# A two-layer attention and feed-forward kernel: first feed-forward on rows sorted by expert, later queries beside the second attention

## The reference

```python
x = x + _L0_xattn_ref(_layernorm(x), ctx_2048, itok, ...)
x = x + _L0_ffn_ref(_layernorm(x), router_w, gate_up_w, down_w, shared_gate_w, shared_up_w, shared_down_w)
x = x + _L1_xattn_ref(_layernorm(x), ctx_2048, wq, bq, wkv, bkv, wp, bp)
x = x + _L1_ffn_ref(_layernorm(x), W_up, W_down, W_gate, W_expert)

def _L0_ffn_ref(...):                       # E = 8 experts, K = 2, I = 128
    shared = silu(x @ shared_gate_w) * (x @ shared_up_w) @ shared_down_w
    top_val, top_idx = top_k(x @ router_w, K)
    probs = zeros_like(logits).at[arange(T)[:, None], top_idx].set(sigmoid(top_val))
    xin = probs.T[:, :, None] * x[None]
    gate, up = split(einsum('etd,edf->etf', xin, gate_up_w), 2, axis=-1)
    return shared + einsum('eti,eid->etd', silu(gate) * up, down_w).sum(axis=0)

def _L1_xattn_ref(x, cond, ...):            # 16 heads of 16
    q = qdq(x) @ qdq(wq).T + bq             # qdq: int8 fake quantisation by row
    ...
```

## Time and profile before

| | us |
|---|---|
| median of 3 runs | 811.05 (809.56 to 811.33) |
| the profiled execution, its own time | 809.53 |
| its span, first to last instruction | 807.6 |
| PE busy | 751.5 (93%) |
| DVE busy | 566.8 (70%) |
| ACT busy | 383.5 (47%) |
| POOL busy | 197.8 (24%) |
| mean granted clock of PE | 0.987 |

### The profile page before, as it was taken

How to read it: one execution, slowest core, us unless ns; L and a number is a source line. 1 busy time by engine, 2 the same in 40 slices (tenths; PEclk the granted TensorE clock), 3 DMA queues, 4 the chain that set the end, 5 groups by cost and what they waited for, 6 DMA issues and landing times.

```text
span 807.6 us, 13086 instructions
## 1 busy us (share of the span) xinstructions
PE 751.5 (93%) x5026; PEld 425.8 (53%) x5027; DVE 566.8 (70%) x1290; ACT 383.5 (47%) x562; POOL 197.8 (24%) x208
## 2 busy tenths in 40 slices
PE   7999899979989889789999999999999999899996
PEld 3445677856556556544444455554455554345434
DVE  3967988633455765687788787767787777887814
ACT  2101434445423233236666666556665566564670
POOL 1397322323721311210400504100505002200000
PEclk9999999999999999999999999999999999999999
DMA  9300001105589143144083391630491810550000
GB/s 294 138 0 1 1 1 27 57 1 185 113 146 138 62 60 47 22 60 79 1 145 40 117 135 16 142 55 2 150 116 62 115 23 1 117 69 14 1 2 13
DMA packets 32473, 55.90 MB, mean 69 GB/s; under 512 B 11572, under 2 KB 20532, under 8 KB 31509
## 3 DMA queue, kind: packets, MB, share of 16 engines
q1 hardware_dynamic: 32408, 55.04, 34.6%
HBM read 42.56 MB, written 12.46 MB: 68 GB/s over the span
## 4 chain that ended last, share of the span: by engine, by line
PE 64%; DVE 23%; issue 6%; POOL 3%; ACT 2%; DMA 1%; SPq 0%; DVEq 0%; POOLq 0%; ACTq 0%
PE ps L1111 12%; PE ps L1000 12%; PE ps L1090 9%; PE ps L888 5%; PE ps L898 5%; DVE small L1679 5%; PE ps L944 3%; PE ps L964 3%; POOL r L623 2%; PE ps L814 2%; PE ps L857 2%; PE ps L845 2%; DVE small L1629 1%; DVE r L1598 1%; DVE r L1605 1%
## 5 line engine op out<-in xcount | busy, mean ns | idle before, releaser
L1679 DVE TENSOR_REDUCE small<-ps 128x1 f32<-128x400 f32 (+1 forms) x512 | 286.0, 573 | 81.5 <-PE ps L1000 75.4
L1490 ACT ACTIVATE r<-ps 128x1024 f32<-128x1024 f32 (+1 forms) x208 | 212.6, 1024 | 89.0 <-PE ps L1090 86.1
L1000 PE MATMUL ps<-r 96*128 96x400 bf16 (+1 forms) x512 | 171.0, 341 | 13.7 <-DVE small L1679 10.9
L651 POOL TENSOR_TENSOR r<-r 128x401 bf16<-128x401 f32 (+3 forms) x96 | 87.8, 949 | 204.3 <-ACT r L1331 203.2
L1111 PE MATMUL ps<-r 128*17 128x256 f32 (+1 forms) x1664 | 130.7, 386 | 2.3 <-ACT r L1490 2.0
L1090 PE MATMUL ps<-r 99*128 99x256 bf16 (+1 forms) x832 | 125.8, 273 | 0.0
L1000 PEld LDWEIGHTS ps<-r 96*128 96x128 bf16 x512 | 49.5, 97 | 125.8 <-DVE small L1679 92.6
L1090 PEld LDWEIGHTS ps<-r 99*128 99x128 bf16 (+1 forms) x832 | 81.4, 99 | 31.5 <-issue 9.3
L944 PE MATMUL ps<-r,hT 128*128 128x512 f32 (+1 forms) x160 | 68.4, 559 | 0.0
L898 PE MATMUL ps<-wkvT,r 128*128 128x256 f32 (+1 forms) x208 | 57.0, 392 | 0.0
L1111 PEld LDWEIGHTS ps<-r 128*17 128x17 f32 (+1 forms) x1664 | 27.7, 95 | 52.0 <-issue 41.4
(11 more groups left out here) (199 smaller groups left out, 966.9 us busy)
## 6 DMA issues: line engine op xcount, KB each, us to landing
r<-kscr SPq DMA_DIRECT2D x96, 200.1 KB, 8.9
kscr<-r SPq DMA_DIRECT2D x24, 400.2 KB, 3.5
r<-in_ctx_dram SPq DMA_DIRECT2D x4, 1601.0 KB, 6.7
r<-qscr SPq DMA_DIRECT2D x24, 128.0 KB, 4.9
r<-in_wo_dram SPq DMA_DIRECT2D x1, 2048.0 KB, 13.5
r<-in_gu_dram SPq DMA_DIRECT2D x1, 2048.0 KB, 7.7
qscr<-qpart SPq DMA_DIRECT2D x24, 64.0 KB, 1.7
x<-in_x_dram SPq DMA_DIRECT2D x1, 1024.0 KB, 5.3
```

Source lines behind the costliest of these rows:

```text
L651: last = nc.gpsimd.tensor_tensor(into[:, a:a + n], kf[s][:, a:a + n], of[:, a:a + n], ALU.subtract)
L1000: mm(bank(ca % 2)[:, 0:m], qst[0:SROWS, h, q0:q0 + P], kst[0:SROWS, s % 2, h % HALF, a:a + m], start=True, stop=True).then_inc(mx_mm, 1)
L1490: fn(pr[i % 3][0:n, :], bank(2 + 2 * (i % 2), 2)[0:n, :], ACT.Exp, scale=SCALE1)\
L1679: v.tensor_reduce(mxc[quad % 2][:, n:n + 1], bank(ca % 2)[:, 0:m], AX_X, ALU.max).then_inc(mx_rdy, 1)
```

## The change

**First feed-forward.** Each row goes to its two experts only. Two groups are sorted apart: tiles 0 and 1, and tiles 2 to 7. For each group PE transposes and routes all its tiles, DVE takes the top two and writes a one-hot membership, PE multiplies it by a triangular matrix and by ones (the rank of each row within its expert, and the counts), and DVE works out each row's two positions in a list where each expert starts at a multiple of 128 (`choose`, `place`). ACT makes two scaled copies of each row, with the sigmoid as scale. POOL scatters them by indirect DMA into a DRAM buffer (`send`) that is cleared at the program's start. The list has 11 and 19 blocks of 128 rows, the most that 256 and 768 rows can need with two experts each, 30 together, and all 30 are always computed. DVE also writes each block's expert times 256 (`owner_at`).

SP loads the blocks in 15 pairs through three buffers (`load_sorted`) and stores results through four (`store_sorted`). The items are those 15 pairs and four shared ones (two tiles each). In step n, PE does gate-up of item n (for a pair after loading the two owners into registers, which select the weights' columns), the transposition of the next pair, the down product of item n-2 and the hidden transposition of item n-1. ACT does silu for both blocks and the copies, DVE the product and the evacuation. A row's two results come back by indirect gathers on POOL (`fetch`), and DVE adds them to x (`join`).

**Queries.** They go by batch. Batch 0's stand beside the items 12 to 16. Those of batches 1, 2 and 3 go into the second attention's table, with joins in steps 0, 4 and 9 and the rest from steps 1, 25 and 77. The values of batch 1 and the first quad's maxima stand beside the steps from 18 and 19 on.

**Keys.** The splits of stages 0 and 1 move from POOL to DVE (three passes of 1601 columns each, in the steps 1 to 4). Their writing and the stacking of quads 0 and 1 move from SP to POOL; the stacking of quads 2 and 3, and the rows of ones, come on SP after the last pair is stored. A reload of the context moves to ACT's queue. Two activation tables are loaded early by one-element instructions.

```diff
+GROUPS = ((0, 2), (2, TILES))
+SORTED = [2 * (b - a) + E - 1 for a, b in GROUPS]
+SFIRST = [0, SORTED[0]]
+NSORT = sum(SORTED)
+PAIRS = NSORT // 2
+ITEMS = [("s", 0)] + [("x", i) for i in range(6)] + [("s", 1), ("s", 2), ("s", 3)] + [("x", i) for i in range(6, PAIRS)]
+NI = len(ITEMS)
+XRING, YRING = 3, 4
+QPARTS = ((0, "q_moments"), (2, "q_variance"), (4, "q_norm"), (5, "q_scale"), (6, "q_round"),
+          (7, "turn_xq"), (8, "project_q"), (10, "turn_q"))
+JOINS = (None, 0, 4, 9)
+QSTEPS = (None, 1, 25, 4 * KT + 25)
+QFIRST = (12, 12, 13, 13, 13, 14, 15, 16)
...
@@ schedule()
+    for b in range(1, B):
+        put(JOINS[b], "query", b, "join")
+    for b in range(1, B):
+        for at, part in QPARTS:
+            put(QSTEPS[b] + at, "query", b, part)
...
@@ @block.sync
+            for i in range(XRING):
+                load_sorted(i)
+            for n in range(NI + 3):
+                if 3 <= n and ITEMS[n - 3][0] == "x":
+                    store_sorted(ITEMS[n - 3][1])
+                if n + 1 < NI and ITEMS[n + 1][0] == "x" and ITEMS[n + 1][1] + XRING < PAIRS:
+                    load_sorted(ITEMS[n + 1][1] + XRING)
+                if n == QFIRST[-1] + 1:
+                    write_queries(0)
+                    stack_queries(0)
...
@@ @block.gpsimd
+            def send(g):
+                a, z = GROUPS[g]
+                pool.wait_ge(place_rdy, 2 * g + 1)
...
+                        nc.gpsimd.indirect_dma_start(xscr[g], bass.IndirectOffsetOnAxis(pos[:, k, t:t + 1], 0),
+                                                     xin[:, k, t, :], None).then_inc(sent[g], 16)
...
+            send(0)
+            sigmoid_power(1)
+            send(1)
+            write_keys(pool, 0)
+            stack_quad(pool, 0)
+            write_keys(pool, 1)
+            stack_quad(pool, 1)
+            fetch(0)
+            rsqrt_query(0)
+            split_queries(0)
+            fetch(1)
+            fetch(2)
+            rsqrt_query(1)
+            fetch(3)
...
@@ @block.tensor
+            def gate_up(n):
+                what, i = ITEMS[n]
+                if what == "x":
...
+                    owners[n] = [pe.value_load(owner_at[0:1, j:j + 1], min_val=0, max_val=(E - 1) * D)
+                                 for j in (2 * i, 2 * i + 1)]
+                    pe.wait_ge(xt_ev, i + 1)
...
+                for t in range(2):
+                    for k in range(FC):
+                        if what == "x":
+                            last = mm(bank(2 + n % 2)[:, t * D:(t + 1) * D], xsT[:, t, k, :],
+                                      gu[:, k, bass.ds(owners[n][t], D)], start=k == 0, stop=k == FC - 1)
...
+            for n in range(FSTEPS):
+                if n < NI:
+                    gate_up(n)
+                if n + 1 < NI and ITEMS[n + 1][0] == "x":
+                    turn_sorted(ITEMS[n + 1][1])
+                if 2 <= n < NI + 2:
+                    weigh_down(n - 2)
+                if 1 <= n <= NI:
+                    turn_hidden(n - 1)
+                beside_first(ASIDE.get(n, []))
...
@@ @block.vector
+            for n in range(FSTEPS):
+                if n < NI:
+                    hidden(n)
+                if 2 <= n < NI + 2:
+                    expert_out(n - 2)
+                for what, *a in ASIDE.get(n, []):
...
+            def query(b, part, between):
...
+                if part == "join":
+                    dve.wait_ge(fetched, 64 * (b + 1))
+                    link(v.tensor_tensor(x2, x2, hT2.rearrange("p t c n -> p t (c n)"), ALU.add))
+                    v.tensor_tensor(x2, x2, y2, ALU.add).then_inc(x_rdy, 1)
...
```

More of the change, by code:

```diff
@@ L993, in max_scores @@
                 if n == 0:
-                    pe.wait_ge(k_stk[quad % 4], 96 * (quad // 4 + 1))
+                    pe.wait_ge(*stacked(quad))
                     pe.wait_ge(q_stk[b], 96)
@@ L1218, in beside @@
                         tail(*a, between)
+                    elif what == "query":
+                        query(*a)
             shift(0)
-            pe.wait_ge(v_ev, NV + 5)
-            values(1, 6, 4)
             for quad in range(QUADS + 2):
```

1115 lines of the change are left out of this document (667 added, 448 removed).

## The result

The changed kernel takes 804.87 us (median of 6 runs, 802.82 to 807.77), the kernel before 809.75 (6 runs beside them): ratio 0.9939, 95% interval 0.9916 to 0.9962. The forecast was 19 us faster, the gain is 5. The profiled execution took 805.29 with a span of 803.2, against 809.53 and 807.6.

A forecast was written before the change was run, and what follows sets the result against it. It took PE as the engine to shorten in the experts, where every tile is multiplied by all eight. 809.5 less 31.1 before the first score plus 12 in the attention gave 790.4 us, range 763 to 824.

The forecast's parts named there:

- First expert product: End of the first feed-forward's front: items start at 215.7 us, 9.4 later than in the kernel before.
- R: Experts, PE's queue ahead of gate-up: two register loads leave 1.5 us uncovered per pair, possible span 0 to 3.9.
- rival 1: Experts: PE runs the register loads hidden under queued matmuls, R = 0, giving 770.9 us; chance 0.18.
- Join of batch 0: Experts, on DVE: due at 257.5 + 8R = 269.5 us, with the gathers in at 264.4, 5 us to spare.
- c: POOL's queue: cost of one transfer, taken as 1.27 us; above 1.42 it delays DVE's join.
- landings: POOL's queue: two landings of 3.5 us for the key transfers, and 2.5 us for the four gathers.
- the first half of the sum: Everything ahead of the second attention's first score: that score comes 31.1 us earlier.
- First maxima: Start of the second attention: 307.1 us, set by the stacked queries, at 287.6 + 13R plus transfers and landings.
- first score: Second attention: 330.7 us against 361.8 before, after 32 maxima at 0.573 and 4.6 us to the score.
- Attention +12: Second attention: moved queries and joins add 12 us, between 5 and 16; first quad 7, third 3, batch 3's 2.
- Rival 2: POOL's queue delays DVE's join: 806.7 us at c = 1.9, an estimated 848 at c = 3.1; chance 0.17.
- Rival 4: Experts: granted clock falls; all 15 pairs at the 1.2 GHz level add 50.7 us, giving 841; chance 0.08.

The follow-up runs named there:

- stack1_late: Changed kernel with the six transfers stacking the second quad's keys issued on POOL behind batch 0's gathers, not ahead; 801.0 us, 0.9878 of the kernel before.
- no_loads: Changed kernel without PE's register loads, each sorted block multiplied by a constant expert, its number modulo eight; 802.2 us, 0.9901 of the kernel before.
- six_loads: Changed kernel with each pair's two register loads done three times, six in a row; 820.1 us, 1.0097 of the kernel before.

## Why the prediction was wrong, point by point

- **First expert product**: 215.7 forecast, 214.72 measured. Right.
- **R, the loads, 1.5 a pair**: 0 while the queue is full, 1.17 once. This was rival 1's mechanism; the 1.97 that bounded it stood over a load and a branch. The term was 22.5 us too large over the 15 pairs, 19.5 of it ahead of the queries' turn, which is the part that the sum used.
- **Join of batch 0 due at 269.5**: it started at 269.21, but by R = 0 it was due at 257.5. The 11.7 us between are a store of 15 us amid POOL's own key transfers; moving six of these gave back some 6 to 9. I had counted POOL's queue (c = 1.27, right for scatters and gathers, 0.51 for the 18 direct transfers) and "landings" of 3.5 us, the median of the kernel before, and 2.5, which no row shows; the gathers took 3.3, and the key writes on POOL's queue 8.7 (median). No term is shown for the landing of the store that the gathers wait for. The error has the same size as the other and hid it: a date that is met does not show its reason. stack1_late and no_loads together do. So the first half of the sum came out (31.1 forecast, 29.3 measured) by luck.
- **First maxima at 307.1, first score at 330.7**: 305.28 and 332.51; the clock cost some 3.9 between them. The queries' turn ended at 288.2, for 271.2 by R = 0: 11.7 of it from the join, the rest behind it, 2 to 3 us of that a pair at half clock (3.78 us for the eight products at 277.87).
- **Attention +12, between 5 and 16**: the step that failed. 24.9 was measured, beyond its bound: 10.9, 2.2, 7.3 and 6.3 in the first, second, third and seventh quads, less 1.6 elsewhere, where I had taken 7, 0, 3 and 2. The first quad I took at 7 for two joins and a batch of queries in DVE's busy time; it cost 10.9, of which the query work 0.5, the joins 8.3, the rest 2.0. The joins' own passes were priced, not the gathers that they wait for, nor that DVE's order puts the maxima behind them. In the third and seventh DVE is not full; PE waits in order for the shared bank (3.1 of 6.3 came back with one step) and its 1.7 us are paid in full, since PE was idle 0.1 us in that quad before. I had read DVE's room in the quads and not PE's.
- **Rival 2, POOL's queue**: c stayed at 1.27 since only one of POOL's 16 scatters met DVE's cast of 1601 columns. The Trainium skill ("SBUF — State Buffer", Who interferes with whom), by which 848 was estimated, has POOL blocked while DVE holds the port pair that they share. The trace agrees where the two met: one scatter took 1.97 us and ended 0.12 after DVE's cast. The estimate of 848 had put all 34 transfers beside such work. The 0.17 us against which the prediction held DVE's 0.86 was another instruction's; the same line (L1655) takes 0.29 elsewhere. But the place that this rival named, DVE's join idle behind gathers, is where the time went, by way of the DMA engines.
- **Rival 4, the clock**: not in the pairs with full queues, but at 0.50 to 0.57 in stretches behind a wait of PE (260, 276, 300, 332).

## What to carry to other kernels

Price work that is moved beside a busy stage by the wait that its consumer will have in order, on every engine that it touches: the idle time of the stage's busiest engine says what is free there, and here it was 0.1 us. A transfer's landing time taken from a quiet stretch says nothing of a stretch in which 2.4 MB of other transfers are queued; add up the bytes of all queues. When a forecast date is met, check its terms apart, since two of mine cancelled.

## What the runs showed of the hardware

- Two register loads in PE's queue cost nothing behind queued products and 0.585 us each in the open; six cost 3.08 and 4.08 us there (six_loads).
- A store of sorted rows, 128 or 256 KB, landed after 2.1 to 17.7 us in the same execution, by what else was queued.
- A scatter or gather holds POOL's queue for 1.27 us, a direct transfer for 0.51 to 0.57. A scatter beside DVE's cast of 1601 columns lasted until 0.11 to 0.12 us after it, in the changed kernel's profile and all 18 others.
- In the changed kernel PE's granted clock stood at 0.50 to 0.57 behind its waits before 261.9, 277.9 and 305.3 and was back at 1.00 by 268, 284 and 316. Not every wait did this: in six_loads it kept 1.00 behind waits of 2.75 and 3.08 us. In the attention it fell in other places from one execution of the same program to the next.
